# xDeepFM forward pass, one core: rows laid out through DRAM, six of 13 row pairs filled by DMA, layer 1 in plain fp32

## The reference, cut to what matters

```python
B, M, V, E, ND = 512, 26, 1250, 32, 13
emb = tables[arange(M), sparse]                       # 512 x 26 x 32
linear_out = lin_sparse_w[arange(M), sparse].sum(-1) + dense @ lin_dense_w
x0 = xk = emb
for w, bb in ((conv1_w, conv1_b), (conv2_w, conv2_b)):        # the two CIN layers, 128 outputs each
    hp = einsum('bhd,bmd->bhmd', xk, x0).reshape(-1, h * M, E)
    xn = sigmoid(einsum('oi,bid->bod', w, hp) + bb[None, :, None])
    xk, half2 = xn[:, :64], xn[:, 64:];  res.append(half2)
cin_out = concatenate(res, 1).sum(-1) @ cin_w + cin_b
h1 = tanh([emb.reshape(-1, 832), dense] @ W1 + b1)            # 845 -> 1024
h2 = tanh(h1 @ W2 + b2);  h3 = tanh(h2 @ W3 + b3)             # 512, 256
return linear_out + cin_out + h3 @ deep_w + deep_b + bias
```

## Time and profile before

| | us |
|---|---|
| median of 3 runs (472.45 to 473.81) | 473.8 |
| the profiled execution | 473.61 |
| its span on the core | 471.8 |
| PE busy | 443.0 (94%) |
| DVE busy | 322.3 (68%) |
| POOL busy | 273.4 (58%) |
| ACT busy | 199.7 (42%) |

### The profile page before, as it was taken

One profiled execution on the slowest core, in us unless ns is written; L12 is line 12 of the kernel. 1 busy time (PEld: TensorE's weight loads), 2 busy tenths in 40 slices (PEclk: granted clock), 3 DMA queues, 4 the chain that ended last, 5 costly groups with the idle time before them and its releaser, 6 DMA issues.

```text
span 471.8 us, 5582 instructions
## 1 busy us (share of the span) xinstructions
PE 443.0 (94%) x2006; PEld 209.7 (44%) x2006; DVE 322.3 (68%) x351; ACT 199.7 (42%) x346; POOL 273.4 (58%) x238
## 2 busy tenths in 40 slices
PE   3574989999999999999999999999999999999998
PEld 3541334343434342434333434334343423888685
DVE  4137757787787888787969797978798687442111
ACT  3063354736464645546363635353546340111111
POOL 6343658685747566666687869686854444930000
PEclk9858899999999999999999999999999999999999
DMA  5100100100000000011102121202110100300000
GB/s 180 14 13 10 15 15 13 15 10 12 9 11 11 10 10 10 11 54 14 51 13 52 15 52 17 50 15 51 26 60 0 46 0 1 124 9 2 0 1 0
DMA packets 21945, 12.04 MB, mean 26 GB/s; under 512 B 17206, under 2 KB 19638, under 8 KB 21918
## 3 DMA queue, kind: packets, MB, share of 16 engines
q1 hardware_dynamic: 17862, 9.87, 7.7%
q0 software_dynamic: 3584, 1.76, 3.2%
q10 hardware_dynamic: 472, 0.05, 0.1%
HBM read 9.96 MB, written 0.00 MB: 21 GB/s over the span
## 4 chain that ended last, share of the span: by engine, by line
PE 77%; DVE 8%; issue 7%; POOL 3%; DMA 3%; SPq 1%; ACTq 1%; ACT 0%; DVEq 0%
PE conv L402 34%; PE conv L380 15%; PE ring L392 10%; DVE prod L668 8%; PE conv L463 7%; PE ring L463 7%; PE ring L365 3%; POOL emb L296 3%; DMA raw<-emb 1%; DMA emb<-in_table,rows 1%; SPq L234 1%; ACTq L234 1%; DMA idx_sb<-in_idx 0%; PE conv L482 0%; SPq L238 0%
## 5 line engine op out<-in xcount | busy, mean ns | idle before, releaser
L668 DVE TENSOR_TENSOR prod<-ring,xk 128x1024 f32<-128x1024 f32 x208 | 242.7, 1217 | 72.2 <-PE ring L392 65.7
L402 PE MATMUL conv<-prod,w_sb 128*64 128x512 f32 x832 | 205.1, 611 | 0.1
L308 POOL TENSOR_TENSOR sq_lo<-sq,sq_hi 117x512 fp32r<-117x512 f32 x88 | 110.5, 1288 | 71.1 <-ACT sq_hi L509 67.9
L296 POOL DMA_INDIRECT emb<-in_table,rows x112 | 110.3, 985 | 52.5 <-issue 29.4
L402 PEld LDWEIGHTS conv<-prod,w_sb 128*64 128x64 f32 x832 | 49.8, 136 | 93.9 <-issue 82.6
L519 ACT ACTIVATE xk<-conv,const_sb 64x512 f32<-64x512 f32 x64 | 43.7, 683 | 107.1 <-PE conv L380 106.3
L392 PE MATMUL ring<-x,sel_sb 58*128 58x512 f32 x416 | 80.8, 456 | 6.2 <-DVE prod L668 3.6
L508 ACT ACTIVATE sq<-ring 117x512 f32<-117x512 f32 x96 | 58.9, 614 | 54.2 <-PE ring L365 53.9
L392 PEld LDWEIGHTS ring<-x,sel_sb 58*128 58x128 f32 x416 | 33.1, 186 | 85.6 <-issue 41.0
L509 ACT ACTIVATE sq_hi<-ring 117x512 fp32r<-117x512 f32 x96 | 59.5, 620 | 0.0
L380 PE MATMUL conv<-sq_hi,w_hi 117*128 117x512 f32 x96 | 42.2, 439 | 0.0
(11 more groups left out here) (78 smaller groups left out, 307.1 us busy)
## 6 DMA issues: line engine op xcount, KB each, us to landing
wpiece<-in_mlp SPq DMA_DIRECT2D x11, 512.0 KB, 3.6
emb<-in_table,rows POOLq DMA_INDIRECT x112, 2.4
raw<-emb SPq DMA_DIRECT2D x93, 16.0 KB
raw<-emb SPq DMA_DIRECT2D x62, 2.0 KB
sel_f<-in_sel SPq DMA_DIRECT2D x1, 832.0 KB, 6.1
const_sb<-in_const SPq DMA_DIRECT2D x1, 658.0 KB, 4.5
w_sb<-in_w SPq DMA_DIRECT2D x1, 416.0 KB, 6.6
wpiece<-in_mlp SPq DMA_DIRECT2D x1, 308.0 KB
```

The source lines that it names most:

```text
L296: pool.indirect_dma_start(out=emb[0:n, i, j, :], out_offset=None, in_=table, in_offset=bass.IndirectOffsetOnAxis(ap=rows[0:n, i, j:j + 1], ...
L308: nc.gpsimd.tensor_tensor(sq_lo[0:UK, u, c, :], sq[0:UK, s % SQR, :], sq_hi[0:UK, u, c, :].bitcast(F32), ALU.subtract).then_inc(lo_done, 1)
L402: mm = nc.tensor.matmul(conv[i % 2][c * HALF:(c + 1) * HALF, :], w2_sb[:, t, :], prod[r % RP][:, c, :], start=(t == 0), stop=(t == T2 - 1))
L668: nc.vector.tensor_tensor(prod[r % RP][:, :, :].rearrange("p c n -> p (c n)"), spread_bank(r)[:, :, :].rearrange("p c n -> p (c n)"), xk[i ...
```

## The change

- **Layout through DRAM.** POOL still issues seven gathers for a pair, now with 32 samples by 4 features in each. `lay_out(i)` is now two DMAs from `emb` to a DRAM tensor `laid`, and `fetch(i)` two DMAs from there to `raw`. The next gather waits for `laid`, not for `raw`.
- **Copied tiles.** Tiles t = 2, 3, 6, 7, 10, 11 have no spread and no ring slot. SP fills one of RC = 5 buffers `copied` by two DMAs that repeat a row of `laid` over 64 partitions; DVE multiplies in place. `prod` has three buffers instead of four.
- **Layer 1** is three plain fp32 matmuls for each half. ACT squares once, into `sq` with two buffers; `low` is gone from POOL and DVE.
- **x_low** of pairs 3 to 15 goes from DVE to POOL, ahead of that round's gather, which now waits for it.
- **GROUPS** have four tiles; SUMS_IN and L1_IN have new places.
- **MLP weights** come in 24 pieces of 512 columns: 14 are split by ACT and DVE during pairs 1 to 14, ten by POOL at the end.

```diff
-GJ = 1 + 2 * NG
+GJ = NG + 1
-RP = 4
-SUMS_IN = ({1: (1, 0), 2: (1, 1), 3: (1, 2)},
-           {0: (1, 0), 1: (1, 1), 2: (1, 2), 6: (2, 0)}, ...
-L1_IN = ({4: 0, 5: 1}, {3: 0, 4: 1}, {2: 0, 3: 1}, {2: 0, 3: 1})
+RP = 3
+COPIED = (2, 3, 6, 7, 10, 11)
+RC = 5
+LAY_AT = 3
+GROUPS = ((0, 1, 2, 3), (4, 5, 6, 7), (8, 9, 10, 11), (12,))
+SUMS_IN = ({1: ((1, 0), (1, 1)), 2: ((1, 2),)},
+           {0: ((1, 0), (1, 1)), 1: ((1, 2),), 3: ((2, 0),)},
+           {0: ((1, 1), (1, 2)), 3: ((2, 0), (2, 1))},
+           {0: ((1, 2),), 2: ((2, 0),), 3: ((2, 1),)})
+L1_IN = ({2: 0, 3: 1}, {1: 0, 2: 1}, {1: 0, 2: 1}, {0: 0, 1: 1})
@@ sync @@
+                sp.dma_start(laid[i, 0:NG * GM, :].rearrange("(j m) (b e) -> (m b) j e", m=GM, e=E),
+                             emb[:, i, 0:NG, 0:E]).then_inc(laid_in[i % RX], 16)
+            def fetch(i):
+                sp.wait_ge(laid_in[i % RX], LAID * (i // RX + 1))
+                for c in range(2):
+                    sp.dma_start(raw[i % RX][HALF * c:HALF * c + M, :], laid[i, :, c * CH:(c + 1) * CH])
+            def copy(n):
+                if n >= RC:
+                    sp.wait_ge(main_done, tile_of_copy(n - RC) + 1)
+                sp.wait_ge(laid_in[i % RX], LAID * (i // RX + 1))
+                for k in range(2):
+                    sp.dma_start(copied[n % RC][HALF * k:HALF * (k + 1), :, :].rearrange("p c n -> p (c n)"),
+                                 laid[i, 2 * t + k, :].partition_broadcast(HALF))
             for i in range(NPAIR):
+                if i < KW:
+                    load_piece(i)
+                for k in range(NC):
+                    n = NC * i + RC + k
+                    if n < NC * NPAIR:
+                        copy(n)
+                    if k == (NC - 1 if i < 2 else LAY_AT) and i + RX < NPAIR:
+                        lay_out(i + RX)
+                    fetch(i + RX)
@@ gpsimd @@
-                        low(i + 1, u)
+                if i and i + 2 < NPAIR:
+                    x_low(i + 2)
+                    pool.wait_ge(x_lo_done, 2 * (i + 3))
                 if i + RX < NPAIR:
                     gather(i + RX)
@@ tensor @@
-                    for k, (w, s) in enumerate(((w1_hi, sq_hi), (w1_lo, sq_hi), (w1_hi, sq_lo))):
+                    mm = nc.tensor.matmul(l1_bank(i, c)[:, :], w1_sb[:, u, :], sq[i % 2][0:UK, u, c, :],
@@ scalar @@
+                    nc.scalar.activation(sq[i % 2][0:UK, u, c, :], sums_bank(i, u)[0:UK, c, :], ACT.Square)
+                if i <= KW:
+                    piece_high(i - 1)
@@ vector @@
+                    if t in COPIED:
+                        dve.wait_ge(copy_in[n % RC], 32 * (n // RC + 1))
+                        left = copied[n % RC]
```

More of the change, by code:

```diff
@@ L58, with build @@
 CONST = SEL1_AT + NPR
-def build(nc, idx, table, dense_t, const, w2, mlp1, mlp2, mlp3, sel2, out):
+def build(nc, idx, table, dense_t, const, w2, mlp1, mlp2, mlp3, sel2, laid, out):
     with ExitStack() as ctx:
@@ L157, in build @@
         rows_in = [sem(f"rows_in{k}") for k in range(GSEM)]
+        laid_in = [sem(f"laid_in{k}") for k in range(RX)]
         raw_in = [sem(f"raw_in{k}") for k in range(RX)]
+        copy_in = [sem(f"copy_in{k}") for k in range(RC)]
         sel_done = sem("sel_done")
@@ L199, in sums_in, with spreads_in, spreads_up_to @@
-            return (i + ahead, u) if ahead and i + ahead < NPAIR else None
+            return [(i + ahead, u) for ahead, u in SUMS_IN[min(i, 3)].get(g, ()) if i + ahead < NPAIR]
+        def spreads_in(i, g):
+            if g + 1 < len(GROUPS):
+                return [T2 * i + t for t in GROUPS[g + 1] if t in SPREAD]
+            return [T2 * (i + 1) + t for t in GROUPS[0] if t in SPREAD and i + 1 < NPAIR]
+        def spreads_up_to(r):
+            return NS * (r // T2) + SPREAD.index(r % T2) + 1
@@ L208, in build @@
             enter(("sums", 0, u))
-        for t in GROUPS[0]:
-            enter(("spread", t))
+        for r in spreads_in(-1, len(GROUPS) - 1):
+            enter(("spread", r))
         for i in range(NPAIR):
             for g in range(len(GROUPS)):
[L213 to L219, removed]
+                for r in spreads_in(i, g):
+                    enter(("spread", r))
+                for j, u in sums_in(i, g):
+                    enter(("sums", j, u))
         def l1_bank(i, c):
@@ L266, in _ @@
             sp.dma_start(w2_sb[:, :, :], w2).then_inc(w2_in, 16)
-            for i in range(RX):
-                lay_out(i)
+            lay_out(0)
+            fetch(0)
+            for n in range(RC):
+                copy(n)
+            lay_out(1)
+            fetch(1)
             sp.wait_ge(zeroed, 1)
@@ L341, in _ @@
             pool.wait_ge(lin_done, 1)
-            for k in range(K1, PIECES):
+            for k in range(KW, PIECES):
                 split_piece(k)
@@ L441, in _ @@
             pe.wait_ge(lin_step, 1)
-            for c in range(2):
-                nc.tensor.matmul(ring[1][0:NPAIR, 1, 0:PB], lin[:, :, c], ind_sb[:, c, :], start=(c == 0), stop=False)
-            nc.tensor.matmul(ring[1][0:NPAIR, 1, 0:PB], emb[0:ML * PB, :, 0, E], ind_sb[0:ML * PB, 2, :],
+            nc.tensor.matmul(ring[1][0:NPAIR, 1, 0:PB], lin[:, :], ind_sb[:, :], start=True, stop=False)
+            nc.tensor.matmul(ring[1][0:NPAIR, 1, 0:PB], emb[0:ML * PB, :, NG, E], ind_sb[0:ML * PB, :],
                              start=False, stop=True).then_inc(lin_done, 1)
```

246 lines of the change are left out of this document (109 added, 137 removed), and 3 rows, old and new, of the table SUMS_IN.

## The result

The changed kernel takes **497.5 us** (median, 495.9 to 502.7) against 473.5 for the kernel before: ratio 1.053, 95% interval 1.049 to 1.057, slower. The profiled execution has a span of 494.1 us, against 471.8. The forecast was 487 us with 471 to 507 as its range: the sign was right and the time inside, but 10 us above the centre, and the sum that led to 487 was not the reason. The ratios in this document are against executions of the kernel before taken beside each version (their medians lie between 471.9 and 473.5), so they are not exactly the quotients of the times shown.

The account below looks back on a forecast made before the run. The prediction took repeated pairs as bound by PE's own work. Profiled 473.6, +16 for the first pairs, -5 for the repeated pairs, +3 for the last pair gave 487.6, predicted as 487 us, range 471 to 507.

Parts of the forecast that it names:

- The repeated pair's work: PE's work in pairs 3 to 14: 21.1 us against 22.1, plus 0.9 waiting, 22.0; -5 us over 12 pairs.
- The wait at the ring: In a repeated pair's first group PE waits 0.8 to 0.9 us at spread 5 for product 1.
- Up to 22 it is hidden: POOL's loop, 19 to 24 us a turn, is hidden up to a turn of 22 us.
- rival (a): A loop through POOL, 19 to 24 us a turn, sets the pairs' period; at 24, 505 us; chance 0.22.
- The first pairs: Start to pair 3: +7 by pair 1's start, pair 1 +3.2, pair 2 +1.2, clock +5; together +16 us.
- The stretches: PE at half clock for one stretch each at the waits ahead of pairs 1 and 2: +5 us (0 to +7).
- The last pair: Bound by DVE, whose copied products each wait 0.4 to 1.3 us for POOL's `xt_lo`: +3 us (0 to +5).
- Copies at nothing: The DMA copies stay hidden: 9 us of a 22 us pair, or some 16 by the skill's page; no cost.
- The sign for rival (a): POOL's `x_low` starting at a drifting phase in the pair, instead of a constant 3 to 5 us in.
- The last sign of being wrong: SP's queue, where layout waits stand ahead of copies, runs late.

Follow-up runs that it names:

- version 9: Changed kernel with `x_low` on VectorE, first pairs reordered, `xt_lo` held back with single waits, and each pair's first main tile ahead of its second spread: 462.5 us.
- versions 7 and 8: Version 2 with the last pair's `xt_lo` held back by product counts: 475.0 us; then also a wait for each `xt_lo` and first pairs reordered: 469.2 us.
- Experiment 10: Layer 1 as nine fp32r matmuls a half again, low parts of squares on GpSimd, in version 2 and in version 9: 476.1 and 473.6 us.
- version 2: Changed kernel with `x_low` of all pairs back on VectorE, so that GpSimd only gathers: 474.0 us, ratio 1.004.
- the first version with fp32r: Version 2 with layer 1 as nine fp32r matmuls a half again, low parts of squares on GpSimd, two squares on ACT: 476.1 us, ratio 1.007.

## Why the prediction was right in sign and wrong in its sum

*The repeated pair's work (predicted 21.1 and a wait of 0.9, 22.0 together).* Measured 20.69 and 0.60, 21.29. Both halves of layer 1 take 5.54, not 5.8. Four main tiles side by side take 3.59 (173.03 to 176.62), 0.897 each; I had carried 0.935 over from groups of two, and twelve of them make 0.46. The wait at the ring was there, at the place predicted, and version 9 shows it was real idle time. Without the loop the term is 255.1 - 268.7 = -13.6, not -5: mis-sized by 8.6 us, with the right mechanism.

*The step that failed: "Up to 22 it is hidden", and with it the choice of the forecast over rival (a).* The prediction gave the loop 19 to 24, a turn of 22.9 lies in it, and every member of its sum was right within 1 us (the stretch on SP's queue and the fetch took 7.4, where 4 to 7 was said). But its forecast left the loop out and gave it a chance of 0.22. It set the limit by its own 22.0 for the pair; the turn of 22.9 is above even that, and with a pair of 21.29 the limit is lower still. The loop cost 277.2 - 255.1 = 22.1 us in pairs 3 to 14. Rival (a) priced it at 18 from its own threshold on. It also named only waits: the two stretches of half clock behind a wait, 3.0 and 2.5 us, were not in it.

*The first pairs (+16, measured +10.5).* The first product starts at 33.92, 2.6 earlier than in the earlier trace rows, where I had 0.5 later: the term was mis-sized by 3 and lay outside its ends (-1.5 and +2). Which of the shorter steps ahead of it (four issues instead of ten, half the squares) gave the gain was not tried apart. Pair 0 then takes 5.3 longer (predicted 6.5), pair 1 5.1 (3.2 and a stretch of clock), pair 2 2.7 (1.2 and a stretch). The stretches came where predicted, ahead of pairs 1 and 2. Timeline of PE at the first:

```profile
71.98 3.68 PE L445 MATMUL conv<-prod,w_sb 128*64 128x512 f32 x8
75.44 2.60 PE L445 MATMUL conv<-copied,w_sb 128*64 128x512 f32 x8
77.97 0.73 PE L435 MATMUL ring<-x,sel_sb 58*128 58x512 f32 x4
```

These four tiles take 5.99, and 5.62 at the second (100.05 to 105.67), against 3.59 in an undisturbed pair: the stretches cost 2.4 and 2.0, near the 2.5 taken for each.

*The last pair (+3, measured +3.4)* was right, and versions 7 and 8 show that the lock between GpSimd's SBUF reads and products with both inputs in SBUF is its cause. The rule of the Trainium skill's page "SBUF — State Buffer", section "Who interferes with whom", that was cited there (the later one stands for the whole of the earlier) agrees, and the traces show both directions: products of 1.15 follow each other at 2.2, and an `xt_lo` of 1.25 (4.99 for four) becomes 1.82 in the mean. Experiment 10 adds that one instruction can stand for a whole row of the other engine's: 7.45 us behind six low parts.

*Copies at nothing.* The rate of the copies never bound the pair: DVE's 15.7 us of waiting for them are gone in version 2 with the same traffic. In the pair from 313.65 to 334.94 the DMA engines are busy 0.74 and move 171 GB/s. That is 231 at a full share, against 349 of the earlier trace rows, so 9 us for a pair's copies was too little: their 3.1 MB make 13.6 at 231, and all of the stretch 15.8 (0.74 x 21.29). The Trainium skill's page "SBUF — State Buffer", section "Door 1: The DMA port swizzle", which gives 196 GB/s at 1 MB for 64 partitions, led to an estimate of some 16 for the copies, nearer than 9. Whether the 64 partitions are the reason of the lower rate was not tried apart. Stretch, span, busy time of PE, PEld, DVE, ACT and POOL, clock, share, GB/s:

```profile
313.65:334.94 21.29, 20.69 (x86) 7.03 (x85) 17.23 (x19) 9.08 (x15) 10.83 (x9) 1.00 0.74 171
```

*Sum without the loop.* 473.6 + 10.5 - 13.6 + 3.4 = 473.9, and version 2, the change without its loop, measured 474.0. That 487 came out within 10 us was luck in part: a gain of 8.6 in the pairs and 5.5 in the first pairs that I did not see stood against 22 of a loop that I saw and did not charge.

*The signs named ahead.* Layer 1 at 2.77 (2.8 to 3.0 was said), the idle ahead of the second spread 0.60 (0.8), starts of pairs 1 to 3 at 72, 100, 125 (76, 105, 130), two more dips. The sign for rival (a) was a drifting phase of `x_low`, where 3 to 5 us into a pair was said: it starts 7.3, 8.9 and 9.8 us into pairs 5, 6 and 7 (180.37, 203.18 and 226.11), and stays near 9.9 in pair 8, where PE waits once a pair for the loop. The last sign of being wrong, copies late on SP's queue behind a layout's wait, came true as well.

## What to carry to other kernels

When work moves to an engine that also feeds the pipeline's start, write down the loop through it (here gather, layout, fetch, high part, low part, next gather), add up one turn, and compare it with the new period: here a turn of 22.9 lay 0.5 above the old period of 22.4, and 1.6 above the new one of 21.3. Where a turn and a period lie within 10% of each other, the cheapest test is to shorten the turn at one member, as putting the fetch ahead of four copy DMAs did for 22 us. And a gain in the first pairs or a cheaper instruction form shows nothing until such a loop is gone, so take the loop out before judging the other edits.

## What the runs showed of the hardware that was not expected

- A gather on GpSimd seems to stand for DVE instructions with both inputs in SBUF as a low part does. It takes 0.94 alone; in the turn above 1.66 beside two copied products and 1.41 beside a low part of DVE, and 2.69 in the first version with fp32r (209.56, beside two copied products and a low part on DVE from 208.53 to 211.47). This is read from the times; no run tried it apart.
- Such an instruction can stand for several of the other engine's in a row. The two `x_low` of 2.62 together took 5.29 in the pair that began at 262.36, the second of them 3.95, beside two copied products and a low part of DVE; that turn of the loop came to 25.9 (gathers at 252.07 and 277.99), and the next pair took 28.06.
- A plain fp32 matmul of 128 output columns and 512 columns takes 2.77 / 3 = 0.92 us, the same as one with a single output column (0.94), and as much as 3.6 fp32r passes of 0.254 (2.29 / 9).
